# A two-layer cross-attention kernel: the Gram's high x low product made once and its transpose added on TensorE, with a new order of work on all engines

## The reference

```
q = x^T Wq^T + bq ; k = Wk ctx + bk ; v = Wv ctx + bv          # q, k have 64 channels
x' = v softmax(q k)^T + x                                      # softmax over 1024
theta = Wth x' + bth ; phi = Wphi ctx + bphi ; g = Wg ctx + bg # 256 channels
y = (theta^T phi / 1024) g ;  out = batchnorm(Wo y + bo) + x'
```

## Time and profile before

| | before |
|---|---|
| median of 3 runs | 1081.09 us (1079.33 to 1081.38) |
| the profiled execution, its time | 1080.8 us |
| its span, first to last instruction | 1079.0 us |
| granted TensorE clock, of full speed | 0.997 |
| busy: TensorE, VectorE, ScalarE, GpSimd | 1052.7, 693.1, 468.9, 286.3 us |

### The profile page before, as it was taken

How to read it: one execution, slowest core, us unless ns; L and a number is a source line. 1 busy time by engine, 2 the same in 40 slices (tenths; PEclk the granted TensorE clock), 3 DMA queues, 4 the chain that set the end, 5 groups by cost and what they waited for, 6 DMA issues and landing times.

```text
span 1079.0 us, 14139 instructions
## 1 busy us (share of the span) xinstructions
PE 1052.7 (98%) x5272; PEld 871.3 (81%) x5272; DVE 693.1 (64%) x929; ACT 468.9 (43%) x794; POOL 286.3 (27%) x198
## 2 busy tenths in 40 slices
PE   6899999999999999999999999999999999999997
PEld 5688878888788887888878888788887888788886
DVE  5985287853878438773487745876367762778625
ACT  7643254433544345443544335443255432545411
POOL 1411243122521226112360124502254022440220
PEclk9999999999999999999999999999999999999999
DMA  7434252352513614136142442424424343233502
GB/s 251 140 73 136 105 177 66 76 173 80 191 41 77 200 59 172 44 90 199 59 157 56 113 163 69 147 68 111 154 78 138 78 112 142 87 129 79 137 20 78
DMA packets 80627, 122.07 MB, mean 113 GB/s; under 512 B 13104, under 2 KB 46384, under 8 KB 80560
## 3 DMA queue, kind: packets, MB, share of 16 engines
q1 hardware_dynamic: 80560, 121.17, 36.4%
HBM read 70.79 MB, written 16.78 MB: 81 GB/s over the span
## 4 chain that ended last, share of the span: by engine, by line
PE 81%; DVE 8%; DMA 5%; SPq 2%; issue 2%; ACT 2%; DVEq 0%; ACTq 0%
PE pG L549 32%; PE pG L469 12%; PE pG L460 10%; PE pG L560 8%; DMA out_dram<-xr 5%; PE pG L489 4%; PE pS L501 3%; DVE xr L862 2%; PE pM L528 2%; PE pM L537 2%; DVE xr L857 2%; PE pT L501 2%; PE pS L439 1%; PE pT L450 1%; PE pT L570 1%
## 5 line engine op out<-in xcount | busy, mean ns | idle before, releaser
L549 PE MATMUL pG<-pt,vT 128*128 128x512 f32 x1536 | 352.6, 389 | 1.2 <-DVE pt L812 1.2
L549 PEld LDWEIGHTS pG<-pt,vT 128*128 128x128 f32 x1536 | 287.3, 188 | 60.3 <-issue 1.3
L460 PE MATMUL pG<-wv,x2s 128*128 128x512 f32 x768 | 179.8, 391 | 0.8 <-DVE vT L765 0.8
L841 DVE SCALAR_TENSOR_TENSOR xr<-pG,cl,xr 128x512 f32<-128x512 f32 x64 | 48.1, 751 | 194.5 <-PE pG L549 190.3
L891 POOL TENSOR_TENSOR xms<-xr,xms 128x512 fp32r<-128x512 f32 x64 | 88.5, 1383 | 312.2 <-ACT xms L698 312.2
L460 PEld LDWEIGHTS pG<-wv,x2s 128*128 128x128 f32 x768 | 143.2, 188 | 30.5 <-DVE vT L765 1.2
L469 PE MATMUL pG<-x2Ts 128*128 128x256 f32 (+2 forms) x768 | 128.9, 327 | 0.0
L469 PEld LDWEIGHTS pG<-x2Ts 128*128 128x128 f32 x768 | 116.6, 191 | 9.6 <-issue 1.4
L698 ACT ACTIVATE xms<-xr 128x512 fp32r<-128x512 f32 x64 | 40.3, 630 | 190.1 <-DVE xr L841 190.1
L883 POOL TENSOR_TENSOR x2Ts<-x2T_f,x2Ts 128x512 fp32r<-128x512 f32 x64 | 92.2, 1472 | 83.8 <-ACT x2Ts L645 83.8
L887 POOL TENSOR_TENSOR ys<-yf,ys 128x256 fp32r<-128x256 f32 x32 | 28.5, 892 | 313.6 <-ACT ys L666 313.6
(11 more groups left out here) (106 smaller groups left out, 1279.5 us busy)
## 6 DMA issues: line engine op xcount, KB each, us to landing
mv<-tp SPq DMA_DIRECT2D x512, 64.0 KB, 2.0
st<-in_ctx_dram SPq DMA_DIRECT2D x32, 512.0 KB, 6.0
x2T_f<-in_ctx2T_dram SPq DMA_DIRECT2D x32, 512.0 KB, 5.8
xr<-in_x_dram SPq DMA_DIRECT2D x64, 256.0 KB, 3.5
out_dram<-xr SPq DMA_DIRECT2D x64, 256.0 KB, 2.7
...
```

The costliest lines, as they stand in the source:

```text
L460: last = mm(bank, x2s[:, l, c, 128 * m:128 * m + 128], wv[:, r, c, :], start=(c == 0 and n == 0), stop=(c == 3 and n == 2))
L549: last = mm(bank, vT[:, l, m, 128 * c:128 * c + 128], pt(h)[:, r, m, :], start=(m == 0 and n == 0), stop=(m == 7 and n == 2))
```

## The change

The Gram's pass LO x HI is the transpose of HI x LO. The changed kernel makes HI x LO once, over all 512 columns, in four new steps `L:0` to `L:3` (8 products each). ScalarE rounds L to float32r into `gram[LO]`. `G:r` is now only HI x HI (8 products), and then for each 128-column block c of the row one product of the L block (c, r) with an identity matrix `ident_r`, which adds the transposed block in PSUM: 4, 3, 2 and 2 such products of 128 columns. VectorE adds L's own row when it reads the bank (`do_G`, into `gram_f`, now four tiles), ScalarE makes HI from that, and VectorE LO in a new step `G2`. Two of the four `gram_f` tiles lie where v:6's and v:7's HI go, so these wait for `G2:3` and `GT:1`. A batch has 32 + 32 + 11 = 75 Gram products in place of 96. All four order tables are written anew; SyncE's program and GpSimd's list are the same but for one copy, of the identity.

```diff
-    k=2, q=2, S=8, GT=2, M=2, B=2, g=36, s_row=1, s_col=1,
+    k=2, q=2, S=8, GT=2, M=2, B=2, g=40, s_row=1, s_col=1,
...
-G_Y, G_PV, G_TH, G_WY = 12, 16, 24, 28
+G_Y, G_PV, G_TH, G_WY = 16, 20, 28, 32
...
+def use_l(b, r):
+    return v_first(b) + r
 def use_g(b, r):
-    return v_first(b) + r
+    return v_first(b) + 4 + r
...
 LATER = dict(
     pe=(
-        "q:0 k:0 k:1 q:1 v:0 v:1 v:2 gs S:0 S:1 gt G:0 G:1 S:2 S:3 GT:0 G:2 G:3 v:3 S:4 S:5 GT:1 v:4 v:5 v:6 v:7 "
+        "gs k:0 k:1 q:0 q:1 v:0 v:1 v:2 S:0 S:1 gt L:0 L:1 S:2 L:2 S:3 L:3 G:0 S:4 G:1 GT:0 G:2 G:3 v:3 S:5 v:4 "
...
     act=(
+        "xs:2 xs:3 s x1:2 x1:3 k x2T:0 x2T:1 x2T:2 q x2T:3 x2T:4 x2T:5 v:0 x2T:6 q2 v:1 k2 x2T:7 gs v:2 gt S:0 "
+        "L:0 L:1 S:1 L:2 S:2 L:3 S:3 G:0 GT:0 G:1 T:0 S:4 v:3 T:1 G:2 G:3 v:4 v:5 T:2 GT:1 v:6 S:5 v:7 T:3 Y:0 "
...
-        gram_f = [at(f"gram_f{i}", [128, 512], F, ra + 28672 + 2048 * i) for i in range(2)]
+        gram_f = [at(f"gram_f{i}", [128, 512], F, ra + (12288 if i >= 2 else 28672) + 2048 * (i % 2)) for i in range(4)]
...
+        def wait_free(eng, b, i):
+            r = i - v_first(b)
+            if 0 <= r < 4:
+                wait(eng, "Lhi", b, r)
+            else:
+                wait(eng, "gf", b, i if r < 0 else i - 4)
...
+            def do_L(b, r):
+                bank = g_bank(b, use_l(b, r))
+                for m in range(8):
+                    wait(eng, "x2Tlo", b, m)
+                    last = mm(bank, x2Ts[:, HI, m, 128 * r:128 * r + 128], x2Ts[:, LO, m, :],
+                              start=(m == 0), stop=(m == 7))
+                done(last, "g")
+
             def do_G(b, r):
                 bank = g_bank(b, use_g(b, r))
                 for m in range(8):
-                    wait(eng, "x2Tlo", b, m)
-                    for n, (u, v) in enumerate(PASSES):
-                        last = mm(bank[:, G_FROM[r]:512], x2Ts[:, u, m, 128 * r:128 * r + 128],
-                                  x2Ts[:, v, m, G_FROM[r]:512], start=(m == 0 and n == 0), stop=(m == 7 and n == 2))
+                    mm(bank[:, G_FROM[r]:512], x2Ts[:, HI, m, 128 * r:128 * r + 128],
+                       x2Ts[:, HI, m, G_FROM[r]:512], start=(m == 0), stop=False)
...
+                for c in range(G_FROM[r] // 128, 4):
+                    wait(eng, "Lhi", b, c)
+                    last = mm(bank[:, 128 * c:128 * c + 128], gram[:, LO, c, 128 * r:128 * r + 128], ident_r[:, :],
+                              start=False, stop=(c == 3))
                 done(last, "g")
...
             def do_GT(b, r):
-                wait(eng, "Gf", b, r)
+                wait_free(eng, b, use_g(b, r))
...
                 wait(eng, "g", b, use_v(b, m))
+                if m >= 6:
+                    wait(eng, "Glo", b, 3)
+                    wait(eng, "GT", b, 1)
...
+                done(act(gram[:, LO, r, :], bank_of(use_l(b, r)), ACT.Copy), "Lhi")
...
             def do_G(b, r):
+                i = use_g(b, r)
+                wait(eng, "g", b, i)
+                done(tt(gram_f[r][:, G_FROM[r]:512], bank_of(i)[:, G_FROM[r]:512],
+                        gram[:, LO, r, G_FROM[r]:512].bitcast(F), ALU.add), "gf")
+
+            def do_G2(b, r):
                 wait(eng, "Ghi", b, r)
-                if r < 2:
-                    wait(eng, "Gf", b, r)
-                done(tt(gram[:, LO, r, G_FROM[r]:512], bank_of(use_g(b, r))[:, G_FROM[r]:512],
-                        gram[:, HI, r, G_FROM[r]:512].bitcast(F), ALU.subtract), "gf")
+                if r >= 2:
+                    wait(eng, "g", b, use_g(b, 3))
+                done(tt(gram[:, LO, r, G_FROM[r]:512], gram_f[r][:, G_FROM[r]:512],
+                        gram[:, HI, r, G_FROM[r]:512].bitcast(F), ALU.subtract), "Glo")
```

More of the change, by code:

```diff
@@ L23 @@
 PER = dict(
-    k=2, q=2, S=8, GT=2, M=2, B=2, g=36, s_row=1, s_col=1,
-    t1k=1, t1q=1, khi=1, qhi=1, vhi=8, exp=8, Thi=8, Ghi=4, Gf=2, GThi=2, Yhi=4, shi=1, s_rowc=1, s_colc=1, mthi=1, Bhi=2,
+    k=2, q=2, S=8, GT=2, M=2, B=2, g=40, s_row=1, s_col=1,
+    t1k=1, t1q=1, khi=1, qhi=1, vhi=8, exp=8, Thi=8, Ghi=4, Lhi=4, GThi=2, Yhi=4, shi=1, s_rowc=1, s_colc=1, mthi=1, Bhi=2,
     xhi=8, thhi=4, x2hi=4, x1hi=4, x2Thi=8,
-    kf=4, qf=2, klo=1, qlo=1, gf=36, mx=8, rec=8, norm=8, tr=8, Tlo=8, GTlo=2, slo=1, gsum=2, mtf=2, mtlo=1, Blo=2,
+    kf=4, qf=2, klo=1, qlo=1, gf=36, mx=8, rec=8, norm=8, tr=8, Tlo=8, Glo=4, GTlo=2, slo=1, gsum=2, mtf=2, mtlo=1, Blo=2,
     x2sum=4, x2lo=4, oa=8,
@@ L152, in xattn_kernel @@
         ident = at("ident", [128, 128], F, o); o += 512
+        ident_r = at("ident_r", [128, 128], R, o); o += 512
         scol = at("scol", [128, 4], F, o); o += 32
@@ L287, in pt_half @@
                     for t in range(2)]
-        grow = gram_f[1][0:2, 0:256]
+        grow = gram_f[2][0:2, 0:256]
         def gram_turned(r):
@@ L422, in g_bank @@
                 if i >= G_WY + 2:
-                    wait(eng, "gf", b, i - 4)
+                    wait_free(eng, b, i - 4)
                 elif i >= G_WY:
@@ L426, in g_bank @@
                 elif i >= 2:
-                    wait(eng, "gf", b, i - 2)
+                    wait_free(eng, b, i - 2)
                 elif b:
-                    wait(eng, "gf", b - 1, G_WY + 6 + i)
+                    wait_free(eng, b - 1, G_WY + 6 + i)
                 return bank_of(i)
@@ L445, in do_q @@
                 if h == 0 and b:
-                    wait(eng, "gf", b - 1, G_WY + 5)
+                    wait_free(eng, b - 1, G_WY + 5)
                 for c in range(4):
@@ L484, in do_Y @@
                 bank = g_bank(b, G_Y + c)
-                wait(eng, "gf", b, use_g(b, 3))
+                wait(eng, "Glo", b, 3)
                 wait(eng, "GTlo", b, 1)
@@ L565, in do_wy @@
                 bank = g_bank(b, G_WY + 4 * h + c)
-                wait(eng, "gf", b, G_TH + 2 * h + 1)
+                wait_free(eng, b, G_TH + 2 * h + 1)
                 wait(eng, "Blo", b, 1)
@@ L572, in do_wy @@
                 done(last, "g")
[L574 removed]
+            do = dict(k=do_k, q=do_q, v=do_v, S=do_S, L=do_L, G=do_G, GT=do_GT, Y=do_Y, gs=do_gs, gt=do_gt, M=do_M, B=do_B, PV=do_PV, th=do_th, wy=do_wy)
             for b, s in order("pe"):
@@ L664, in do_Y @@
             def do_Y(b, c):
-                wait(eng, "gf", b, G_Y + c)
+                wait_free(eng, b, G_Y + c)
                 done(act(ys[:, HI, c, :], yf[:, c, :], ACT.Copy), "Yhi")
@@ L696, in do_PV @@
             def do_PV(b, h, c):
-                wait(eng, "gf", b, G_PV + 4 * h + c)
+                wait_free(eng, b, G_PV + 4 * h + c)
                 done(act(xms(h)[:, c, HI, :], xr[c][:, :], ACT.Copy), "xhi")
@@ L735, in do_x2, with do_x2T @@
                 done(tt(x2s[:, LO, c, :], st2(c)[:, :], x2s[:, HI, c, :].bitcast(F), ALU.subtract), "x2lo")
+            def do_x2T(b, m):
+                wait(eng, "x2Thi", b, m)
+                if b:
+                    wait(eng, "g", b - 1, G_WY + 7)
+                done(tt(x2Ts[:, LO, m, :], x2T_raw(m), x2Ts[:, HI, m, :].bitcast(F), ALU.subtract), "x2Tlo")
             def do_x1(b, c):
@@ L898, in _ @@
                               pattern=[[-1, 128]], channel_multiplier=1).then_inc(s_id, 1)
+            eng.wait_ge(s_id, 3)
+            eng.tensor_copy(out=ident_r[:, :], in_=ident[:, :]).then_inc(s_id, 1)
             eng.wait_ge(s_cd, 16)
```

24 lines of the change are left out of this document (12 added, 12 removed), and 52 rows, old and new, of tables (act, dve, pe).

## The result

The changed kernel takes 1065.3 us (median of 4 runs, 1062.81 to 1068.98) against 1080.21 us (4 runs, 1078.89 to 1081.38) for the kernel before: a ratio of 0.9865, 95% interval 0.9833 to 0.9897. In a second group of runs it took 1063.82 us (5 runs) against 1082.17 us, 0.9841 (0.9815 to 0.9866). The forecast was 1066.5 us. The sum came out; its single terms did not, as the rows show.

What follows compares the result with a forecast made beforehand. TensorE's own stream, busy 98% of the span, was taken as the bound. Gram -5.7, waits +1.6, boundary -7.7 and first batch -2.5 sum to -14.3 us: 1080.8 to 1066.5 us, range 1054 to 1074.

Steps and rivals of the forecast that it cites:

- The Gram: TensorE's Gram products: 3.20 us a batch saved before paying eleven identity products; -5.7 us over eight batches.
- the price of an identity product: TensorE's 128-column identity products: taken at the 512-column pitch, 0.2267 us each, not at the transpose row's 0.10 us.
- The waits that come in: New waits from S:0 to PV, such as identity products on ScalarE's L:3: 0.2 us a batch, +1.6 us.
- rival 2: Identity products are cheap (0.10 us): 11.1 us less, 1055.4 us, though part may become PV's wait for T:3; chance 0.25.
- The boundary: From wy to the next S:0: new order regains 1.1 of 1.6 us lost at each of seven boundaries, -7.7 us.
- The walk: ScalarE and VectorE traced op by op at the boundary: q's copy 424.1, klo 431.4, S:0 near 431.5 instead of 432.53.
- the output transfer of 8.05 us: At the old boundary qhi, ahead of qlo and klo, waited for this transfer, queued behind four x2T loads.
- rival 3: The new order gives nothing: collisions move, x2T loads still hold output transfers; only the Gram's 5.7 us stay, 1075; chance 0.15.
- The first batch: Batch 0: v:4 fills the hole before exp S:0 and consts come earlier, against later sums; net -2.5 us.
- the signs named beforehand: Identity pitch 0.22 to 0.24 us, 168 products fewer, first out op 0.7, boundary 27.8, S:0 to PV 42, first L 39.9.

Runs made afterwards that it cites:

- a_merge: The changed kernel with S:2 put behind L:2, next to S:3, on TensorE in batches 1 to 7: 1067.31 us (one run).
- a_slate: The changed kernel with the split of the sums moved behind out:1,1 on VectorE and gs behind q on TensorE: 1059.61 us, ratio 0.98.
- b_newbound: The kernel before, its Gram and order inside a batch kept, with the changed kernel's order at the batch boundary alone: 1074.85 us, ratio 0.9928.
- a_oldbound: The changed kernel with the old order at the batch boundary, its Gram and batch 0 order kept: 1072.32 us, ratio 0.991.

## Why the prediction was right in its sum, and where it was wrong

**The Gram.** The step that failed is the price of an identity product: "I take the upper price, as the cheap row belongs to another instruction and the size alone does not make them alike". The cheap row was the right one: 0.085 to 0.12 us in the stream, 1.11 us for all eleven, 0.114 us marginal. I had weighed a rule of the Trainium skill against it, "FP8 and Floating Point Precision", section "TensorE Precision Notes", four passes for FP32; no float32r product of 128 columns shows such a thing here. Its "TensorE: Matmul & The Clock Gate", section "Back-to-back issue gap", 81 ns at 128 columns, stands near that, and the trace agrees with it roughly. Yet the stage gained not 1.4 us more a batch but 0.4 more than forecast (0.90 against 0.51), as three things went against it: L costs 7.82 us, not 7.25 (each of its groups begins behind another kind of product, which I take for the cause); HI x HI 5.36, not 5.23; and four single score rows cost 0.89 to 0.90 us each where a pair had cost 1.59, so 0.4 us in all. 3.20-1.11-0.57-0.13-0.4 = 1.0 us, near the 0.90 measured. Of the two reasons given, that single rows of scores cost more than pairs is measured; that L's longer pieces have the same cause is argued. I had counted products and not the places where their kind changes.

**The waits that come in.** +1.6 us forecast, none measured in the later batches: L:3 was in time by 0.9 us (1.0 worked out), and no TensorE wait for it stands in the profile; the 43.10 us of batch 2 are the clock. a_merge shows that the margin can be used up: a later exp of S:2 makes the wait. PV did not wait for T:3 in the later batches either, the objection to rival 2. In batch 0 it did, 1.0 us, and 1.2 us in the kernel before:

```profile
PE pG L573 <- DVE pt L852: 1.0, 1, 1.0
```

**The boundary.** "1.1 us of the 1.6 is regained: 7 x 1.1". In four boundaries more is regained, 1.2 to 1.4 us; in three of seven nothing. The step that failed is the walk with one set of transfer times: it took the loads as given once issued. The walk had q's copy over 20.4 us after wy's start and S:0 at 27.8. In the boundary of 27.45 us q's copy is over at 20.4 as well; at the end of batch 2 it is over at 21.7, as x2T:2 ahead of it waits for a load that lands 6.62 us after its issue, and S:0 comes at 28.9. The loads were issued 0.1 to 0.6 us sooner against wy's start (12.8 to 13.3 against 13.4), not 1 us, but for the first boundary, whose table has no split of the sums ahead of out:0,1: there they are issued at 11.2, and it lasts 27.6 to 27.7 us in all eight profiles with that order and SyncE's program unchanged.

The walk also missed that the split of the sums (`sst`), moved ahead of out:0,1, falls on GpSimd's x1 split and stretches from 0.15 to 2.3 us. I had quoted the rule for that, the Trainium skill, "SBUF — State Buffer", section "Who interferes with whom", and applied it to the big ops only. The trace agrees with it down to four columns: two SBUF inputs are enough. The first out op took 0.74 us, as forecast.

I had also read the kernel before as bound by the output transfer of 8.05 us there. Its seven boundaries do not follow it: `qhi` starts 24.1 to 24.8 us after wy's start, and `klo` at 27.0 in all seven, as `qlo` beside GpSimd's splits takes 1.9 us when early and 1.2 when late. That rival 3's mechanism (loads that hold the output transfer) is at work in the long boundaries is supported by the chains, beside a load that holds q's copy and a `qlo` that is stretched; that lost slack is what exposes them is shown by a_slate.

**The first batch.** -2.5 forecast, -4.4 at S:0 and -5.4 at the first PV, of which the Gram's term is 0.5: the term was half of what came. I had priced the constants by their own 1.29 us and the hole behind S:1. VectorE's order did more: `klo` went ahead of q, where GpSimd is idle and it takes 0.68 us and not 1.66, and `qlo`, which begins while GpSimd is idle, 1.22 us and not 2.31. Another part is TensorE's clock. I had counted G:0 and G:1 of batch 0 as slow without asking why; before, they ran behind the hole of 2.38 us, and the clock was at its lower level for the first part of them:

```profile
40.67:44.08 3.41, 3.41 (x11) 2.18 (x10) 3.38 (x4) 3.07 (x4) 0.15 (x1) 0.50 0.00 0
```

and with v:4 in that place the changed kernel runs the same part of the batch at the full clock:

```profile
37.10:43.90 6.80, 6.26 (x27) 4.35 (x26) 6.73 (x7) 5.83 (x7) 2.30 (x2) 1.00 0.02 5
```

3.41 us at 0.50 instead of 1.00 are 1.7 us, an estimate, as far as TensorE was the limit there. b_newbound, whose batch 0 keeps the old hole, has the same fall (39.78 to 43.20 us).

Of the signs named beforehand, the 168 products fewer and the first out op came; the identity products were cheap, the first L stood at 37.1 us and not 39.9, S:0 to PV took 41.6 and not 42, and S:0 followed `klo` with the boundary at 28.3 us on the mean and not 27.8.

So the forecast of -14.3 us met -15.2 because errors of both signs cancelled, which is luck: the Gram and its waits 1.7 us better (with 1.5 us of clock against them), the first batch 1.9 and the end 0.8 better, the boundaries 3.5 worse. The end was not in the forecast; it came with the new order at the boundary, as b_newbound has it (16.5 us) and a_oldbound not (17.2). The chance given to rival 3, 0.15, was too small for what its mechanism does in nearly half of the boundaries, and rival 2 was right in its price and wrong in its total.
